# Sliding-window attention stage of a two-layer megakernel: probabilities scaled ahead of their transposes, GELU over two items, new slot table

## The reference, cut to what matters

```
for i in range(6):
    x = attn_layer(shift_tokens(x), Wqkv[i], q_scale[i], k_scale[i], Wo[i]) + x
    x = ffn_layer(shift_tokens(x), ln_g[i], ln_b[i], W1[i], b1[i], W2[i], b2[i]) + x
# attn_layer: 16 heads of 64; q, k, v = split(x @ Wqkv); q, k = l2norm(.) * scale, then rotary
#   window 32: each query sees its own window and the one before
sim  = where(mask, -max, (q @ k.T) * 8);  attn = softmax(sim, -1)
out  = attn @ v;                          return out @ Wo
# ffn_layer: xn = layernorm(x); a, gate = split(xn @ W1 + b1)
return a * gelu(gate) @ W2 + b2
```

## Time and profile before

| | us |
|---|---|
| runs (3) | 5466.16, 5465.18, 5457.78 |
| median | 5465.18 |
| the profiled execution | 5452.7 |
| its span, first to last instruction | 5450.9 |

### The profile page before, as it was taken

How to read it: one execution, slowest core, us unless ns; L and a number is a source line. 1 busy time by engine, 2 the same in 40 slices (tenths; PEclk the granted TensorE clock), 3 DMA queues, 4 the chain that set the end, 5 groups by cost and what they waited for, 6 DMA issues and landing times. The chain is left out here.

```text
span 5450.9 us, 109430 instructions
## 1 busy us (share of the span) xinstructions
PE 5026.2 (92%) x34408; PEld 3517.0 (65%) x34408; DVE 4764.0 (87%) x8649; ACT 4045.7 (74%) x11685; POOL 3152.2 (58%) x2280
## 2 busy tenths in 40 slices
PE   6997899999999999999999999999999999688887
PEld 4664667767667676666767666676667777444543
DVE  4666899999899998999989999899999999398897
ACT  2554688888788887888778888788888788577764
POOL 0001766666666666666666666666666666144444
PEclk9998999999999999999999999999999999788887
DMA  1000000000000000000000000000000000000000
GB/s 22 6 5 20 7 1 1 0 6 15 2 0 0 6 15 2 0 1 4 17 2 0 1 1 21 2 0 1 0 14 3 0 1 0 5 3 3 3 3 5
DMA packets 35461, 26.80 MB, mean 5 GB/s; under 512 B 11203, under 2 KB 29190, under 8 KB 35078
## 3 DMA queue, kind: packets, MB, share of 16 engines
q1 hardware_dynamic: 26302, 22.22, 1.4%
q10 hardware_dynamic: 8776, 0.45, 0.1%
HBM read 20.56 MB, written 2.10 MB: 4 GB/s over the span
## 5 line engine op out<-in xcount | busy, mean ns | idle before, releaser
L1246 POOL TENSOR_TENSOR b_w<-b_w,b_vt 128x512 f32<-128x512 f32 x768 | 981.5, 1278 | 1292.6 <-DVE b_vt L1155 659.0
L1250 POOL TENSOR_TENSOR b_rn<-b_ssm,all_neg_half 128x16 f32<-128x16 f32 x384 | 1127.6, 2936 | 32.0
L1072 ACT ACTIVATE b_PT<-ps 128x512 f32<-128x512 f32 x768 | 463.7, 604 | 432.8 <-PE ps L927 411.1
L1054 ACT ACTIVATE b_Pr<-ps,b_nm 128x128 f32<-128x128 f32 x1536 | 565.8, 368 | 209.8 <-DVE b_nm L1181 207.9
L1181 DVE TENSOR_REDUCE b_nm<-ps 128x4 f32<-128x640 f32 x768 | 630.7, 821 | 103.3 <-PE ps L907 94.4
L975 PE MATMUL ps<-b_Whi,b_xlo 128*128 128x512 f32 x1152 | 586.0, 509 | 40.8 <-DVE b_vt L1155 24.5
L1056 ACT ACTIVATE b_Pr<-ps,b_nm 128x160 f32<-128x160 f32 x1536 | 611.9, 398 | 0.0
L1153 DVE TENSOR_TENSOR b_w<-ps,until_b_rotab 128x512 f32<-128x512 f32 x768 | 529.2, 689 | 55.0 <-ACT b_sq L1087 40.2
L1087 ACT ACTIVATE b_sq<-ps 128x512 f32<-128x512 f32 x768 | 469.2, 611 | 82.7 <-PE ps L977 82.1
L1155 DVE TENSOR_TENSOR b_vt<-ps,until_b_rotab 128x512 f32<-128x512 f32 x768 | 522.9, 681 | 0.0
L1157 DVE TENSOR_REDUCE b_ss<-b_sq 128x8 f32<-128x512 f32 x768 | 519.4, 676 | 0.0
(11 more groups left out here) (269 smaller groups left out, 12585.9 us busy)
## 6 DMA issues: line engine op xcount, KB each, us to landing
b_Wraw<-in_L_ffn_Wqkv SPq DMA_DIRECT2D x36, 256.0 KB, 2.8
b_Wo<-in_L_ffn_Wo SPq DMA_DIRECT2D x6, 512.0 KB, 4.7
a_xtok<-in_L_attn_hidden_states SPq DMA_DIRECT2D x16, 128.0 KB, 2.1
out<-c_xout SPq DMA_DIRECT2D x16, 128.0 KB, 1.8
b_W<-in_L_ffn_W SPq DMA_DIRECT2D x6, 341.0 KB, 3.0
setup_wmod<-in_L_wmod SPq DMA_DIRECT2D x2, 384.0 KB
...
```

Of the source, the lines that this page charges most:

```text
L1054: nc.scalar.activation(s.Pr[:, p % 2, j, 0:P], ps[:, S_BANK[j], WIN:KEYS], ACT.Exp, bias=s.nm[:, h, 0:1], accum_out=s.ssum[:, h, 0:1])
L1246: nc.gpsimd.tensor_tensor(rows, rows, s.vt[:, i % 4], ALU.add).then_inc(s.pool_add, 1)
L1250: nc.gpsimd.tensor_tensor(s.rn[:, j], s.ssm[:, j], g.neg_half[:, 0:HB], ALU.pow).then_inc(s.pool_r, 1)
```

## The change

- The probabilities themselves are divided by their sum, pair by pair. Two slots after a pair's scores DVE inverts the four sums of each row (two heads, two token halves: L1211) and multiplies the far part of the probabilities (the second token half, 2 x 160 columns, L1214); POOL multiplies the near part (2 x 128, L1266). The spreading, its transpose, its copy and the product with rb are gone; ACT copies the output to oT (L1091, semaphore ocopied).
- The transposes of the probabilities move from lag 2 to lag 4, the values from lag 4 to 6, and values now stand right behind the scores; Pr has four buffers for two.
- GELU is taken in odd steps only, over two items' gates in one instruction; the gate product, W2 and the last residual come a step later ("closing"), and there is one more step at the end.
- Three uses of `tensor_scalar` with a factor of 1 or with mean and rstd become forms with two tensors: the input split, the parameter copy lnp, and the layer norm's scaling, which is parted in a subtraction (behind the statistics) and a product.
- The slot table is new, and so is the order within a slot on all four engines.

```diff
-QK_SLOT = {0: (0, 0), 1: (0, 2), 4: (1, 0), 5: (1, 2), 8: (0, 1), 9: (0, 3), 10: (1, 1), 11: (1, 3)}
+QK_SLOT = {0: (0, 0), 2: (0, 2), 4: (1, 0), 5: (1, 2), 7: (0, 1), 9: (0, 3), 11: (1, 1), 12: (1, 3)}
...
-PAIR_T, PAIR_PV = 2, 4
-SPREAD_LAG, TURN_LAG, KEEP_LAG, SCALE_LAG = 4, 5, 4, 7
+PAIR_T, PAIR_PV = 4, 6
+INVERT_LAG, NEAR_LAG, BEFORE_LAG, COPY_LAG = 2, 2, 5, 9
...
-RES_SLOT, STATS_SLOT, NORMED_SLOT, END_SLOT, SPLIT_SLOT = 5, 9, 14, 14, 3
+RES_SLOT, STATS_SLOT, NORMED_SLOT, END_SLOT, SPLIT_SLOT = 7, 11, 13, 15, 6
...
-GELU_SLOT, RSTD_SLOT, GATE_SLOT = 11, 10, 11
+GELU_SLOT, RSTD_SLOT, GATE_SLOT = 12, 13, 13
...
 # PE
-                        for p in range(2):
-                            for tt in range(TT):
-                                last = nc.tensor.transpose(ps[:, T_BANK, p * NT + tt * P:p * NT + (tt + 1) * P],
-                                                           s.rrep[:, tt, 2 * p:2 * p + 2].rearrange("p j e -> p (j e)"), g.ident[:])
-                        last.then_inc(s.rb_full, 1)
...
+                        pe.wait_ge(s.far_scaled, HPAIRS * item + p + 1)
+                        wait(pe, s.pt_ready, HPAIRS * item + p)
+                        for j in range(2):
+                            nc.tensor.transpose(ps[:, T_BANK, j * NT + P:(j + 1) * NT], s.Pr[:, p % 4, j, OWN], g.ident[:])
+                        pe.wait_ge(s.near_scaled, HPAIRS * item + p + 1)
+                        for j in range(2):
+                            last = nc.tensor.transpose(ps[:, T_BANK, j * NT:j * NT + P], s.Pr[:, p % 4, j, 0:P], g.ident[:])
+                        last.then_inc(s.t_done, 1)
...
 # ACT
-                        nc.scalar.activation(s.rb[:], ps[:, T_BANK].rearrange("p (a t) -> p a t", a=2), ACT.Copy).then_inc(s.rb_ready, 1)
+                        nc.scalar.activation(s.oT[:, 2 * i:2 * i + 2], ps[:, O_BANK].rearrange("p (a t) -> p a t", a=2), ACT.Copy).then_inc(s.ocopied, 1)
...
-                        nc.scalar.activation(s.hgate[:], s.hgate[:], ACT.Gelu).then_inc(s.gelu_done, 1)
+                    if step.ffn is not None and step.odd and slot == GELU_SLOT:
...
+                        nc.scalar.activation(s.hgate[:], s.hgate[:], ACT.Gelu).then_inc(s.gelu_done, 2)
...
 # DVE
-                nc.vector.tensor_scalar_mul(s.xhi[lower, parity], own, 1.0)
+                nc.vector.tensor_tensor(s.xhi[lower, parity], own, own, ALU.max)
...
+    nc.vector.tensor_tensor(src[:], src[:], ln.mv[:, :, 0:1].broadcast_to((P, TT, P)), ALU.subtract).then_inc(ln.moment, 1)
+    nc.vector.tensor_tensor(src[:], src[:], ln.rstd[:].rearrange("p (t o) -> p t o", o=1).broadcast_to((P, TT, P)), ALU.mult).then_inc(ln.normed, 1)
...
-                        nc.vector.tensor_tensor(s.oT[:, 2 * i:2 * i + 2], ps[:, O_BANK].rearrange("p (a t) -> p a t", a=2), s.rb[:],
-                                                ALU.mult).then_inc(s.onorm, 1)
...
-                        nc.vector.tensor_tensor(s.rrep[:], wide, wide, ALU.max).then_inc(s.rrep_ready, 1)
...
+                        nc.vector.reciprocal(s.rinv[:, heads], s.ssum[:, heads]).then_inc(s.rinv_ready, 1)
+                        dve.wait_ge(s.rinv_ready, HPAIRS * item + p + 1)
+                        far = s.Pr[:, p % 4, :, P:]
+                        nc.vector.tensor_tensor(far, far, s.rinv[:, heads, 1:2].broadcast_to((P, 2, KEYS)), ALU.mult).then_inc(s.far_scaled, 1)
...
 # POOL
+                        pool.wait_ge(s.rinv_ready, HPAIRS * item + p + 1)
+                        near = s.Pr[:, p % 4, :, 0:P]
+                        nc.gpsimd.tensor_tensor(near, near, s.rinv[:, 2 * p:2 * p + 2, 0:1].broadcast_to((P, 2, P)), ALU.mult).then_inc(s.near_scaled, 1)
```

More of the change, by code:

```diff
@@ L959, in body @@
-                    if step.front is not None and slot in TRANSPOSE_SLOT:
-                        transpose_qk(f, TRANSPOSE_SLOT[slot])
+                    if slot == W2_SLOT and (step.closing is not None or step.vacant):
+                        bank = take_spare(("w2", 0))
+                        if step.vacant:
+                            pe.wait_ge(s.w2_in, 32)
+                        else:
+                            pe.wait_ge(s.w2_in, 32 * step.closing[0] + 32)
+                            pe.wait_ge(s.hg_ready, u)
+                        for c, (_, width) in enumerate(FF_CHUNKS):
+                            last = nc.tensor.matmul(bank[:, 0:NT], s.W2[0:width, c], s.ha[0:width, 1 - pa, c], start=c == 0, stop=c == 2)
+                        give_spare(("w2", 0), last)
@@ L1209, in body @@
[L1209 to L1216 removed]
+                    item, p = pair_at(step, slot, BEFORE_LAG)
```

314 lines of the change are left out of this document (159 added, 155 removed).

## The result

The changed kernel takes 5493.4 us (median of 5 runs, 5490.2 to 5495.4), the one before 5466.2 beside it (5 runs): a ratio of 1.005, 95% interval 1.0035 to 1.0064. In a later comparison it took 5491.8 against 5453.9, ratio 1.0063 (1.0046 to 1.008). So the change makes this kernel slower by about 0.5%. The forecast was 5305 us and its range ended at 5480 us: both the sign and the range were wrong.

What follows compares the result with a forecast made beforehand. PE and DVE, nearly full, wait by turns. PE's 38.3 + 0.7 + 0.55 + 0.4 + 1.0 = 40.95 us an item, 1.65 less; 5452.7 - 157 + 3 = 5299, raised towards the median to 5305 us; range 5150 to 5480.

Steps and rivals of the forecast that it cites:

- PE's own need: PE's work per steady item without waits: 40.5 us before, 38.3 us after the rrep groups go and values follow scores.
- No wait at rrep, new ones at slots 13 and 14: Sign to look for: PE's rrep wait gone, stalls of 0.7 and 0.55 us ahead of the projections of slots 13 and 14.
- elsewhere PE finds its inputs ready: Outside the two tight places PE was to have no new stalls; values and transposes get two slots more slack.
- DVE's work without blocking: DVE per item: 10.9 us off, 7.9 on, so 39.7 becomes 36.7 us if nothing blocks.
- the rival of a late POOL: POOL's queue delays PE's transpose of pair 6 by one slot, 1 us more: 41.95 us an item, 5400 us; chance 0.09.
- What blocks DVE: DVE products of two SBUF tensors wait out wide POOL operations: 14 starts, 4.7 us at random times, half taken, 2.3 us.
- How much of it reaches PE: Of 2.3 us of DVE blocking per item, DVE's idle takes in 1.3 and 1.0 reaches PE.
- about no change: blocking as at random times, 4.7 us: Rival: DVE blocked 4.7 us with 1.1 of other idle, 42.5 us an item, 5460 us; chance 0.08.
- The slower rival: Every far product on DVE waits out POOL's addition, 6.2 us, the layer norm's product 1.1: 5630 us; chance 0.15.
- GELU: its 0.4 us: ACT's block from first table load to first exponential costs PE 0.7 us ahead of scores in odd items, 0.4 on average.
- Layer changes "stay": The five layer changes, some 8 us each above steady steps, were to cost the same after the change.
- The extra step: The added step at the end brings a gate product, W2 and a residual, some 3 us.

## Why the prediction was wrong

The forecast was 154 us below the profiled time of before and it came out 41 above: 195 us. By the sum and the table above, 160 of them are the steady items, 32 the layer changes, 3 the start.

- **PE's own need: right.** With the interval at each wait cut back to the shortest between like matmuls, an item needs an estimated 38.0 us after and 40.6 before (38.3 and 40.5 in the working). The rrep groups and the values behind the scores brought 2.6 together where 2.2 was forecast; no run tells them apart.
- **No wait at rrep, new ones at slots 13 and 14: right; "elsewhere PE finds its inputs ready": wrong.** The rows below have 0.46 of idle each; from start to start it is 0.70 and 0.62 to 0.71, against 0.7 and 0.55 forecast. But by the same count PE loses 4.7 us an item, where the sum has 2.65 in all. The other 3.4 are ahead of other projections, which wait for DVE's rotation, and ahead of the scores. This is where DVE's lateness reaches PE.

```profile
2542.96 0.60 PE L900 MATMUL ps<-all_ident,b_w 128*128 128x128 f32 x4
2544.02 0.50 PE L959 MATMUL ps<-b_Whi,b_xlo 128*128 128x512 f32 x1 [0.46 <-DVE b_vt L1179]
...
2545.88 0.51 PE L959 MATMUL ps<-b_Whi,b_xlo 128*128 128x512 f32 x1 [0.46 <-DVE b_vt L1179]
```

- **DVE's work without blocking: right.** 36.7 forecast, an estimated 35.75 found.
- **POOL: right in size.** 34.2 forecast, 35.8 busy in the item read; PE has no wait for L1266 in the 3600 us, so the rival of a late POOL is out. "It is hidden", though, was wrong: without it the item is 1.1 us shorter.
- **What blocks DVE: this step failed.** 2.3 us forecast, 5.7 found. The working had the mechanism, the starts and POOL's durations, and gave 4.7 for random times; then I halved it, between 4.7 and the "luck of before, 0", with no row for the half. The far products did just what the forecast said (mean 0.22 above the bare time, "some 0.2" written). The other starts, one each an item, stand at a fixed phase to POOL, and there luck is all or nothing: L285 meets the gate product in every item (1.82 us at the least), and lnp behind it meets the addition in every item. The six such starts of the forecast cost 3.9 us, where the random rate of 0.33 gives them 2. The trace of before had shown three such waits; nothing had moved POOL's operations away from them.
- **How much of it reaches PE: failed too.** I let DVE's idle take in 1.3 of 2.3 us. But 35.75 of work, 5.7 of waiting and 1.25 of idle are the 42.7 us: with 5.7 the engine is close to full, and what blocks it reaches the pace: without the near product DVE waits 1.1 us less and the item is 1.1 us shorter. The rival that did hold is the one named "about no change: blocking as at random times, 4.7 us", with 42.5 us an item; I gave it 0.08. By the sum as it stood it should have been the forecast. That it hit the item's time is partly luck, since the random rate was too low for the six and too high for the eight. The slower rival (every far product behind an addition) didn't happen: about one far product in three starts within an addition, and one in four loses 0.7 or 1.0 us.
- **GELU: its 0.4 us is 0.** Taking the loads away altogether moves neither kernel's item. The sign "the waits ahead of the scores grow" did come, 46.5 to 90.4 us in 3600, but the loads aren't its cause, since without them it is 95.5.
- **Layer changes "stay": failed.** They cost 6.3 us more each, 31.6 in all, and turn an even result into a slower one. I had costed the last slots' work for the steady item only, not for the one step in which the next layer's weights queue behind it. What the trace shows there is a stall of 4.1 us for 1.0, a second one of 3.1 us, and a stretch at the lower clock behind the first.
- **The extra step: right.** 3 us forecast, 2.9 found.

The Trainium skill (page "SBUF — State Buffer", section "Who interferes with whom") says that a vector instruction with two SBUF inputs contends with a GpSimd instruction that reads SBUF, for an exclusive lock, and that on this chip a reduction never contends. The trace agrees on both where POOL adds or multiplies: 1.84 us for L285 and 1.23 for a lnp of two numbers, against 0.14 for lnp as a reduction. At an estimated 5.7 us of it an item, this rule was the case against this change. Of the power, which has its inputs in SBUF too, the trace shows no such hold on what starts within it. L1188 at 2550.97, two SBUF inputs, takes 1.22, its mean in the whole stage, inside a power that runs from 2549.99 to 2553.11, and the 166 far products that start within a power have their bare 0.49. There the measurement decides.
